# Adapter weights loaded in 1 KB runs by quarters of output rows, the main loop turned by half a period, and a new order of the first two and the last sequence

## The reference, cut to what matters

```python
w = weight[adapter_ids]                        # 16 adapters of 1024 x 1024, one for each of 8 sequences
y = jnp.einsum('bij,bkj->bik', x, w)           # x: (8, 256, 1024), f32
h = _layernorm(y, gamma, beta)
h = _dyn_quant_linear(h, w1, b1)               # fake int8: round(h / s) * s by row, the same of w1
h = jax.nn.gelu(h, approximate=False)
h = _dyn_quant_linear(h, w3, b3)
return x + h
```

## Time and profile before

| What | Value |
| --- | --- |
| Time, median of 3 runs (lowest, highest) | 408.69 us (406.43, 411.79) |
| Profiled execution, its own time and its span | 405.16 us, 403.3 us |
| Granted TensorE clock, mean | 0.954 |
| TensorE busy | 340.1 us, 84% |
| VectorE, GpSimd, ScalarE busy | 292.8, 266.8, 237.7 us |
| DMA | 67.35 MB, mean 167 GB/s |
| Loop periods p = 3 to 6 on TensorE | 161.73 to 317.78 us |

### The profile page before, as it was taken

One profiled execution on the slowest core, in us unless ns is written; L12 is line 12 of the kernel. 1 busy time (PEld: TensorE's weight loads), 2 busy tenths in 40 slices (PEclk: granted clock), 3 DMA queues, 4 the chain that ended last, 5 costly groups with the idle time before them and its releaser, 6 DMA issues. The chain is left out here.

```text
span 403.3 us, 5528 instructions
## 1 busy us (share of the span) xinstructions
PE 340.1 (84%) x1760; PEld 229.2 (57%) x1760; DVE 292.8 (73%) x348; ACT 237.7 (59%) x248; POOL 266.8 (66%) x160
## 2 busy tenths in 40 slices
PE   3999883988558847899999999999999899992973
PEld 3788663656445533566666666566556566741331
DVE  1489693998776354699768986997689886457457
ACT  2345593858866343786687667756775865214360
POOL 1406334657900647996999699968996899585454
PEclk9999999799888969999999999999999999996898
DMA  7999999964840519999985896689569801300004
GB/s 258 364 265 298 222 283 235 212 160 142 171 105 0 138 20 244 215 191 233 269 154 104 248 250 126 156 257 204 110 156 271 197 0 54 119 37 2 0 27 181
DMA packets 78619, 67.35 MB, mean 167 GB/s; under 512 B 3078, under 2 KB 71686, under 8 KB 78602
## 3 DMA queue, kind: packets, MB, share of 16 engines
q1 hardware_dynamic: 78602, 67.14, 68.9%
HBM read 58.74 MB, written 8.39 MB: 166 GB/s over the span
## 5 line engine op out<-in xcount | busy, mean ns | idle before, releaser
L1080 PE MATMUL a_ps<-w_hi,x_hi 128*128 128x512 f32 x240 | 104.3, 435 | 10.8 <-DVE w_lo L807 8.1
L1129 PE MATMUL f_ps<-w_q,q_t 128*128 128x512 bf16 x416 | 94.3, 380 | 4.9 <-ACT q_t L580 2.7
L1081 PE MATMUL a_ps<-w_lo,x_hi 128*128 128x512 f32 x240 | 96.6, 402 | 0.0
L1082 PE MATMUL a_ps<-w_hi,x_lo 128*128 128x512 f32 x240 | 96.5, 402 | 0.0
L801 DVE STREAM_TRANSPOSE t_ps<-w_nat 128x1024 f32<-128x1024 f32 x56 | 67.3, 1236 | 19.4 <-DMA w_nat<-in_L_cond_weight 19.0
L807 DVE TENSOR_TENSOR w_lo<-t_ps,w_hi 128x1024 fp32r<-128x1024 f32 x56 | 66.9, 1216 | 12.9 <-ACT w_hi L537 12.6
L537 ACT ACTIVATE w_hi<-t_ps 128x1024 fp32r<-128x1024 f32 x56 | 57.1, 1024 | 23.5 <-DVE t_ps L801 22.5
L1129 PEld LDWEIGHTS f_ps<-w_q,q_t 128*128 128x128 bf16 x416 | 38.7, 98 | 55.1 <-issue 4.7
L1080 PEld LDWEIGHTS a_ps<-w_hi,x_hi 128*128 128x128 f32 x240 | 47.1, 196 | 23.9 <-DVE w_lo L807 9.0
L1082 PEld LDWEIGHTS a_ps<-w_hi,x_lo 128*128 128x128 f32 x240 | 46.8, 195 | 10.7
L1081 PEld LDWEIGHTS a_ps<-w_lo,x_hi 128*128 128x128 f32 x240 | 47.2, 197 | 8.7
(11 more groups left out here) (143 smaller groups left out, 488.8 us busy)
## 6 DMA issues: line engine op xcount, KB each, us to landing
w_nat<-in_L_cond_weight SPq DMA_DIRECT2D x112, 256.0 KB, 5.5
x_nat<-in_x SPq DMA_DIRECT2D x28, 256.0 KB, 8.1
x_res<-in_x SPq DMA_DIRECT2D x7, 1024.0 KB, 6.9
out<-o SPq DMA_DIRECT2D x14, 512.0 KB, 2.9
w_nat<-in_L_cond_weight SPq DMA_DIRECT2D x4, 512.0 KB, 6.5
...
```

Source lines behind the costliest of these rows:

```text
L1080: pe.matmul(ps, hi, w_hi[:, u, c], start=begin, stop=False)
L1081: pe.matmul(ps, hi, w_lo[:, u, c], start=False, stop=False)
L1082: last = pe.matmul(ps, lo, w_hi[:, u, c], start=False, stop=end)
L1129: last = pe.matmul(ps[:, half, :], q[:, c, :], w[:, c, half_of(half)], start=c == 0, stop=c == CB - 1)
```

## The change

**Loads.** A unit of loading is now a quarter u of the output rows (256 rows, `LOADED`) with all 1024 inputs, in runs of 256 floats, 1 KB. It is still 1 MB in four DMAs and two triples (transpose, hi, lo); k now names the half ch of the inputs. A TensorE piece of half kh and input half ch therefore reads what loads 2*kh and 2*kh+1 gave, and waits for the `w_lo` of the second of them.

**Loop.** It runs over p = 2 to 6 and begins half a period later in the order: units 2 and 3 of p with ffn1 of p-1, then units 0 and 1 of p+1 with ffn2 of p-1. Each engine's cyclic order inside it is as before, but for SyncE, where load_residual comes first and the stores stand between load_unit(p+2, 0), load_unit(p+2, 1) and the end.

**First sequences.** All 16 tiles of w1 and w3 are rounded on GpSimd. Loads, maxima, transposes of tiles, and the work of sequences 0 to 2 stand in a new order; ffn2 of sequence 0 is done ahead of the loop.

**Last sequence.** Units 2 and 3 of sequence 7 and two FFNs (6 and 7) are left; products are cut in halves of 8 matmuls with transposes between them; round_h and the last round_g of sequence 7 go from VectorE to ScalarE.

The pieces of the diff below are, in this order, the sizes, load_unit, the waits and the place of a unit, SyncE's period, SyncE's and GpSimd's first sequences, and TensorE's piece.

```diff
-    NK = 2
-    CP = CU // NK
-    PIECES = UNITS * NK
+    CP = CU // 2
+    LOADS = 4
+    PIECES = LOADS * CH
...
-    KB = BANK // BLK
+    LOADED = D // LOADS
+    KB = LOADED // BLK
...
-                    src = weight[bass.ds(adapter, 1), kh * BANK:(kh + 1) * BANK, j0:j0 + JQ]
+                    src = weight[bass.ds(adapter, 1), u * LOADED:(u + 1) * LOADED, q * JX:(q + 1) * JX]
...
+        def wait_unit_used(eng, b, kh, ch):
+
+            if ch == 0:
+                eng.wait_ge(w_used, KH * b + kh + 1)
             else:
+                eng.wait_ge(y_done, UNITS * b + TT * kh + TT)
+
+        def part_of_unit(w, u, k):
+
+            kh, quarter = divmod(u, LOADS // KH)
+            return w[:, CH * kh + k, :, quarter * LOADED:(quarter + 1) * LOADED]
...
             def period(p):
-                load_unit(p + 1, 0)
-                load_unit(p + 1, 1)
-                store(p - 2, 0)
+                load_residual(p - 1)
                 load_unit(p + 1, 2)
-                store(p - 2, 1)
-                load_residual(p - 1)
                 if not (isinstance(p, int) and p + 2 > LAST):
                     load_x(p + 2)
                 load_unit(p + 1, 3)
+                if not (isinstance(p, int) and p + 2 > LAST):
+                    load_unit(p + 2, 0)
+                store(p - 1, 0)
+                if not (isinstance(p, int) and p + 2 > LAST):
+                    load_unit(p + 2, 1)
+                store(p - 1, 1)
...
             load_unit(1, 2)
             load_x(2)
-            load_prep(range(9, 13))
+            load_prep((13,))
             load_unit(1, 3)
-            load_prep(range(13, 14))
+            load_prep((14, 11))
             load_unit(2, 0)
+            load_prep((15, 12))
             load_unit(2, 1)
...
             low_x(1, 0)
-            low_x(1, 1)
-            round_prep((4, 5))
+            round_prep((4, 5, 6, 7, 8))
             normalisers_of(0)
+            low_x(1, 1)
...
-                else:
-                    pe.wait_ge(w_lo_ready, piece_no(b, u, k) + 1)
+                elif k == 0:
+                    pe.wait_ge(w_lo_ready, piece_no(b, 2 * kh + 1, ch) + 1)
```

More of the change, by code:

```diff
@@ L365, in _ @@
             store(0, 1)
-            load_residual(1)
-            load_unit(3, 2)
-            load_x(4)
-            load_unit(3, 3)
-            with sp.Fori(3, LAST - 1) as p:
+            with sp.Fori(2, LAST - 1) as p:
                 period(p)
@@ L447, in period @@
             def period(p):
-                add_b1(p - 2, 1)
-                for t in range(TT):
-                    scale_and_shift(p - 1, t)
-                for t in range(TT):
-                    finish(p - 2, t)
                 low_x(p + 1, 0)
@@ L457, in period @@
                 low_x(p + 1, 1)
+                add_b1(p - 1, 1)
+                for t in range(TT):
+                    scale_and_shift(p, t)
+                for t in range(TT):
+                    finish(p - 1, t)
             pool.memset(ident[:], 0.0).then_inc(consts_zeroed, 1)
@@ L482, in _, with residual_last @@
             add_b1(0, 0)
+            round_prep((9, 10, 11, 12))
+            add_b1(0, 1)
             low_x(2, 1)
+            round_prep((13, 14, 15))
             normalisers_of(1)
-            add_b1(0, 1)
+            residual(0)
             scale_and_shift(1, 0)
-            residual(0)
             scale_and_shift(1, 1)
             finish(0, 0)
-            low_x(3, 0)
             finish(0, 1)
-            low_x(3, 1)
-            add_b1(1, 0)
-            residual(1)
-            normalisers_of(2)
-            with pool.Fori(3, LAST) as p:
+            with pool.Fori(2, LAST) as p:
                 period(p)
+            def residual_last(t):
+                pool.wait_ge(x_last_loaded, 16)
+                pool.tensor_tensor(x_last[:, t], x_last[:, t], b3_row, ALU.add).then_inc(x_last_ready, 1)
             f = LAST - 1
-            add_b1(f - 1, 1)
-            for t in range(TT):
-                scale_and_shift(f, t)
-            finish(f - 1, 0)
             pool.wait_ge(mean_var_ready, TT * LAST + 1)
@@ L507, in _ @@
             normalisers(LAST, slice(0, 1))
-            finish(f - 1, 1)
-            residual(f)
+            residual_last(0)
             pool.wait_ge(mean_var_ready, TT * LAST + 2)
@@ L633, in period @@
                 split_x(p + 1, 1)
+                normalise(p, 0)
+                normalise(p, 1)
+                split_w(p + 1, 2, 0)
+                take_g(p - 1, 0)
+                gelu(p - 1, 1)
+                split_w(p + 1, 2, 1)
+                round_g(p - 1, 1)
+                scale_ffn2(p - 1, 0)
+                round_h(p, 0)
+                split_w(p + 1, 3, 0)
+                take_g(p - 1, 1)
+                split_w(p + 1, 3, 1)
+                round_h(p, 1)
+                copy_y(p + 1, 0)
+                scale_ffn2(p - 1, 1)
             def both(b, u):
-                for k in range(NK):
+                for k in range(CH):
                     split_w(b, u, k)
@@ L784, in _ @@
+            scale_ffn2(0, 1)
+            with act.Fori(2, LAST) as p:
+                period(p)
             last_period()
@@ L902, in period @@
                 mean_and_variance(p)
+                rescale1(p - 1, 1)
+                both(transpose_w, p + 1, 2)
+                low_w(p + 1, 2, 0)
+                scales_g(p - 1, 1, a[:, 1, :], 1)
+                low_w(p + 1, 2, 1)
+                scales_h(p, 0, 0)
+                both(transpose_w, p + 1, 3)
+                scales_h(p, 1, 1)
+                both(low_w, p + 1, 3)
+                statistics(p + 1, 0)
             def last_period():
@@ L1124, in transpose_g, with product_half @@
                 transpose_tile(a[:, t, :], f_ps[:, 0], g_transposed)
+            def product_half(q, w, ps, half, done):
+                for c in range(CB):
+                    last = pe.matmul(ps[:, half, :], q[:, c, :], w[:, c, half_of(half)], start=c == 0, stop=c == CB - 1)
+                last.then_inc(done, 1)
             def product(q, w, ps, done):
                 for half in range(KH):
-                    for c in range(CB):
-                        last = pe.matmul(ps[:, half, :], q[:, c, :], w[:, c, half_of(half)], start=c == 0, stop=c == CB - 1)
-                    last.then_inc(done, 1)
+                    product_half(q, w, ps, half, done)
             def ffn1(f, t):
@@ L1204, in period @@
                 ffn1(p - 1, 1)
+                piece(p + 1, 0, 0)
+                transpose_g(p - 1, 0)
+                piece(p + 1, 0, 1)
+                ffn2(p - 1, 0)
+                piece(p + 1, 1, 0)
+                transpose_g(p - 1, 1)
+                piece(p + 1, 1, 1)
+                ffn2(p - 1, 1)
             def last_period():
@@ L1219, in unit @@
+                    pe.wait_ge(w_lo_ready, piece_no(LAST, LOADS - 1, ch) + 1)
+                    if ch == 0:
+                        pe.wait_ge(y_copied, UNITS * LAST + t + 1)
+                    for k in range(2):
+                        last = products(u, t, k, a_ps[:, t, :])
                     if ch == CH - 1:
                         last.then_inc(y_done, 1)
-                unit(0, 0)
-                transpose_g(f - 1, 0)
-                unit(1, 0)
-                ffn2(f - 1, 0)
```

591 lines of the change are left out of this document (239 added, 352 removed).

## The result

The changed kernel takes 393.34 us (median of 4 runs, 390.79 to 396.13) beside 409.07 us for the kernel before on the same chip: ratio 0.962, 95% interval 0.951 to 0.972. It is faster, but by 16 us and not by the 40 that were forecast, and it lies outside the range of 357 to 390. The profiled execution took 391.29 us, with a span of 389.5.

The account below looks back on a forecast made before the run. TensorE, busy 340.1 of 403.3 us, fills the loop; loads and order leave gaps before it. Start 113.5, loop 194.5 and end 58 give 366 us of span, 368 with 1.9 around it, 369 forecast for the median; range 357 to 390.

Parts of the forecast that it names:

- 1 KB runs: Adapter loads: longer runs raise 215 GB/s to 366, so a 1.05 MB load unit takes 2.9 us instead of 4.9.
- rival 3: Adapter loads: 512 bytes were already at line rate, loads stay at 4.9 us, 377 us in all; chance 0.05.
- 215 GB/s again: DMA rate while adapter loads fill the queues: the sign named for rival 3, against above 330 if right.
- Before the loop: From the start to TensorE's entry into the loop: 113.5 us, this part being worth 29 us.
- the walk: New order followed, engine by engine, with trace durations: loop entered at 110.4 us; for the end, 55 us.
- allowance of 3 us: Added before the loop for idle gaps and half-clock matmuls, 110.4 to 113.5; another 3 us at the end.
- The loop: Five periods in the old cyclic order at 38.9 us each: 194.5 us, bounds 190.2 and 200.
- Rival 4: Loop: load_unit(p+2, 1) behind store(p-1, 0) lands late; each us beyond 13 from issue costs five, over 417 us; chance 0.03.
- Rival 1: Before the loop: GpSimd's 13 large operations and the late order cost 1 us each, 382 us in all; chance 0.17.
- rival 2: Loop: stall at the second output half, 3.6 us a period, 18 in all, giving 387 us; chance 0.10.
- The end: From the loop's end to the span's end: 58 us, against 66.2 us in the old kernel.
- the 53 to 62: From the loop's end: us named as a sign that the forecast is right.

Follow-up runs that it names:

- The loads alone: Loads of 8 MB in eight forms without computation, against no kernel: 32 partitions moved 214 to 219 GB/s, 128 moved 349 in 1 KB runs and 290 in 512 byte runs.
- wide loads: Changed kernel with every 256 KB adapter and x load written over all 128 partitions, other elements at a place: 372.89 us, ratio 0.910 to the kernel before.
- the load ahead: Changed kernel with the loop's load_unit(p+2, 1) put before store(p-1, 0) in SyncE's queue: 386.71 us, ratio 0.947 to the kernel before.

## Why the prediction was wrong

- **The step that failed is "1 KB runs": a load unit "takes 2.9 us instead of 4.9".** At 218 GB/s it takes 4.8. The 366 GB/s came from a window in which only DMAs over 128 partitions ran (`w_first`, tiles), the 215 from one in which they write 32. The two windows differed in two things, run length and number of partitions, and the text named the first. The loads alone show that the second is what counted: 219, 214 and 218 GB/s at 32 partitions, 349 at 128. The sign that the prediction named for its rival 3, "215 GB/s again", is what came. A window of the old kernel would have shown it, since its x is loaded in 1 KB runs on 32 partitions; this one, from 23.5 to 27 us, had not been read:

```profile
23.50:27.00 3.50, 3.50 (x21) 2.95 (x21) 2.81 (x4) 1.03 (x1) 0.00 (x0) 1.00 1.15 219
```

The 366 was a mean besides: in the old kernel the adapter of sequence 0, in runs of 1 KB over 128 partitions, moved 349 GB/s from 12 to 17 us, and the tiles of w1, in runs of 4 KB, 408:

```profile
18.00:22.00 4.00, 4.00 (x28) 3.55 (x27) 3.87 (x4) 1.45 (x2) 0.00 (x0) 1.00 1.03 408
```

- **What it cost.** With the rate that the step assumed, the kernel takes 372.9 us against the forecast's 369: of the 24 us, 20 are this term. It is no fixed price of the rate: another order of the same slow loads takes back most of it (380.12 us; by ratio 0.918, beside 0.910 with wide loads).
- **Before the loop** 113.5 was forecast, 129.4 came, and 117.7 with wide loads. So some 12 of the 16 us are the rate, and some 4 the walk, whose allowance of 3 us was too small. The start is not measured to better than some 3 us: the changed kernel and the run with the load ahead have the same start and reached the loop at 129.4 and 132.7. The walk's own marks, without the allowance, against the starts on TensorE:

| Mark | Walk | Wide loads | Changed kernel |
| --- | --- | --- | --- |
| Sequence 1, first piece | 47.3 | 48.0 | 55.0 |
| Sequence 1, unit 2 | 61.3 | 63.5 | 73.4 |
| ffn1 of sequence 0 | 67.4 | 69.6 | 81.3 |
| ffn2 of sequence 0 | 97.3 | 103.2 | 116.9 |
| Loop | 110.4 | 117.7 | 129.4 |

With wide loads the walk holds to 2.2 us until ffn1, and loses most of the rest between ffn1 and ffn2. There it let GpSimd go on from 72 us; in the trace VectorE's rescaling for the first add_b1 stood behind a transpose that waited 2.29 us for `w_nat`, so add_b1 began at 76.5, and the roundings behind it waited another 1.83 for VectorE's scales. How much of the 4 us each of these is was not tried.
- **The loop** was put at 38.9 a period; 39.9 came, 38.5 with wide loads and 38.2 with the load ahead. The longest period, 41.6, also held a second wait of VectorE for `w_nat` (1.00 us at 189.51) and one of TensorE for `q_t` (1.64 at 195.02). Rival 4 had the mechanism, a load behind a store, and mis-sized it: it counted on 13 us from issue to a wait of TensorE, 7 until VectorE wants the load and 6 until `w_lo` is missed. VectorE wanted it 6.1 us after the issue, it landed 7.7 after, and TensorE waits not for `w_lo` but for the rescaling that VectorE does behind the transposes, which has no 6 us of cover.
- **Rival 3** had the loads at 4.9 us, for a wrong reason (512 bytes as line rate), and gave 377. It priced slow loads at 8 us, from late landings of two loads; VectorE waited eight times, and the price was 20. The Trainium skill's rule on 512 bytes (DMA: Bandwidth & Descriptors, Specifications) gives 512 bytes as the smallest transfer at line rate, by which 1 KB gains nothing; at 32 partitions the runs agree (214 and 219 GB/s), at 128 they don't (290 and 349). The 215 against 366 that the prediction holds against the rule compares 32 partitions with 128, and says nothing of it.
- **Rival 1** (GpSimd) and **rival 2** (the second output half) did not occur. GpSimd's large operations between 82 and 129 us took 2.35 to 2.42 us each and its roundings 1.2, as in the sum, and what moving roundings to ScalarE did is above. Whether GpSimd carries the path from there to the loop, as the walk had it, is not settled: in the wide-loads trace VectorE's row maximum at 105.53 waited 4.54 us for it. TensorE has no wait of 0.3 us or more for `w_lo` in the loop.
- **The end** was put at 58: 60.7, and 59.1 to 59.3 in nearly all other runs. It lies in the 53 to 62 that the prediction named, but 1 to 3 us over a sum that had its 3 us of allowance in it: the walk of 55 was 4 to 6 short.
- **A reading.** The prediction takes 0.50 us at 62.03 for a matmul at half clock. Only the 0.79 at 71.15 is one: the granted clock is 0.50 from there to 73.00, but 1.00 from 62.03 to 65.05. A piece's first matmul takes 0.50 at the full clock too, as at 220.17. The allowance of 3 us leaned on both.
